# A vision layer's last image: the other image's tail on two banks, with a table of half-steps for each engine

## The reference

```
q, k, v = x Wq + bq, x Wk + bk, x Wv + bv
h = prelu((gamma * (q k^T)) v Wo + bo)            # no softmax
xm, gate = split(h W_in + b_in)                    # 128 each
xc = silu(xm W_conv + b_conv);  B, C = split(xc W_bc + b_bc)   # 16 each
dt = softplus(xc W_dt + b_dt)
scan over t, for 128 channels x 16 states:  s = exp(dt A) s + dt B xc ;  y = sum_states(C s)
h = layernorm(h + (y * silu(gate)) W_out + b_out)
# 16 groups of 64 tokens per image; each group has one of 16 experts and a shared one
f = relu(h Wi + bi);  twice: f = relu(f (W_expert + W_shared) + biases + f)
h = layernorm(h + f Wo + bo)
```

## Time and profile before

| | us |
|---|---|
| median of 3 runs | 341.44 (341.2, 341.44, 349.24) |
| profiled execution | 342.13 |
| its span | 339.7 |
| PE / PEld busy | 282.3 (83%) / 162.2 (48%) |
| DVE busy | 262.1 (77%) |
| ACT busy | 190.8 (56%) |
| POOL busy | 259.4 (76%) |
| DMA | 85.88 MB, mean 253 GB/s |
| TensorE's mean granted clock | 0.934 of full |

### The profile page before, as it was taken

One profiled execution on the slowest core, in us unless ns is written; L12 is line 12 of the kernel. 1 busy time (PEld: TensorE's weight loads), 2 busy tenths in 40 slices (PEclk: granted clock), 3 DMA queues, 4 the chain that ended last, 5 costly groups with the idle time before them and its releaser, 6 DMA issues. The chain is left out here.

```text
span 339.7 us, 4780 instructions
## 1 busy us (share of the span) xinstructions
PE 282.3 (83%) x1478; PEld 162.2 (48%) x1478; DVE 262.1 (77%) x287; ACT 190.8 (56%) x298; POOL 259.4 (76%) x136
## 2 busy tenths in 40 slices
PE   8898839875678689989797799997855999779996
PEld 5423412433336233356473243565644579458764
DVE  2565678998778988998898899987998799269420
ACT  3004831336895451679946525789377686657322
POOL 1028057999899989998998979989999999949300
PEclk9999957999698799999999799997898999979999
DMA  7970495686689997766799977668999999767000
GB/s 244 415 283 0 145 307 223 215 267 234 244 275 327 309 319 301 268 227 243 263 323 327 312 274 291 205 248 275 296 311 344 346 359 373 268 170 243 21 0 15
DMA packets 47128, 85.88 MB, mean 253 GB/s; under 512 B 7936, under 2 KB 24832, under 8 KB 46848
## 3 DMA queue, kind: packets, MB, share of 16 engines
q1 hardware_dynamic: 46704, 84.43, 73.9%
q10 hardware_dynamic: 400, 1.17, 1.1%
HBM read 75.62 MB, written 1.57 MB: 227 GB/s over the span
## 5 line engine op out<-in xcount | busy, mean ns | idle before, releaser
L1212 POOL TENSOR_TENSOR hc<-h,c_row 128x1024 f32<-128x1024 f32 (+1 forms) x79 | 154.6, 1967 | 22.4 <-DVE h L1341 19.4
L1201 POOL TENSOR_TENSOR ub<-u,b_row 128x1024 f32<-128x1024 f32 (+1 forms) x49 | 98.2, 2004 | 13.0 <-DVE u L1387 11.3
L925 ACT ACTIVATE decay<-delta,neg_a 128x512 f32<-128x512 f32 (+1 forms) x64 | 51.2, 811 | 62.6 <-DVE h L1341 62.2
L664 PEld LDWEIGHTS acc_y<-pack,hc 128*128 128x128 f32 x512 | 61.3, 147 | 39.3 <-issue 23.9
L664 PE MATMUL acc_y<-pack,hc 128*128 128x128 f32 x512 | 74.6, 286 | 3.1 <-POOL hc L1212 3.1
L1341 DVE TENSOR_TENSOR_SCAN h<-decay,ub 128x512 f32<-128x512 f32 (+1 forms) x41 | 66.0, 1610 | 14.4 <-ACT decay L925 7.3
L606 PE MATMUL work<-q,kT 64*128 64x512 f32 x112 | 36.0, 722 | 16.8 <-DVE mixed L1367 12.5
L1367 DVE TENSOR_TENSOR mixed<-gam,work 128x512 f32<-128x512 f32 x56 | 35.5, 676 | 7.2 <-PE work L606 6.6
L952 ACT ACTIVATE decay<-u 128x512 f32<-128x512 f32 (+1 forms) x42 | 26.4, 639 | 21.5 <-DVE h L1341 21.3
L617 PE MATMUL acc_r<-mixed,v_sb 128*64 128x512 f32 x128 | 37.0, 659 | 1.1 <-DVE mixed L1367 1.0
L1341 DVE TENSOR_TENSOR_SCAN h<-decay_own,decay 128x512 f32<-128x512 f32 (+1 forms) x23 | 34.5, 1498 | 1.1
(11 more groups left out here) (210 smaller groups left out, 357.9 us busy)
## 6 DMA issues: line engine op xcount, KB each, us to landing
b_row<-bc_dram SPq DMA_DIRECT2D x64, 512.0 KB, 5.1
c_row<-bc_dram SPq DMA_DIRECT2D x64, 512.0 KB, 5.8
group_w<-expert_w SPq DMA_DIRECT2D x48, 128.0 KB, 4.7
gam<-gammaT SPq DMA_DIRECT2D x8, 512.0 KB, 10.1
expert_w<-routed_w SPq DMA_DIRECT2D x1, 2048.0 KB, 17.9
gam<-expert_w SPq DMA_DIRECT2D x16, 128.0 KB, 5.3
x_in<-xT SPq DMA_DIRECT2D x4, 256.0 KB, 9.0
pack<-packed ACTq DMA_DIRECT2D x1, 788.0 KB, 6.5
```

Of the source, the lines that this page charges most:

```text
L664: mm = nc.tensor.matmul(acc_y[:, to:to + P], hc[:, at:at + P], ident, start=(job.state == 0 and c % 4 == 0), stop=(job.state == STATES - 1 ...
L925: op = nc.scalar.activation(target, delta[:, job.image % 2, columns], ACT.Exp, scale=neg_a[:, job.state:job.state + 1])
L1201: nc.gpsimd.tensor_tensor(ub[:, ring(made, job.halves)], u[:, job.image % 2, tokens(q)], b_row[:, ring(job.at, job.halves)], ALU.mult).the ...
L1212: nc.gpsimd.tensor_tensor(hc[:, here], h[:, here], c_row[:, here], ALU.mult).then_inc(hc_ready, job.halves)
```

## The change

Image 2 is now called `BESIDE`. Its tail leaves `last_steps` and gets a table for each engine: which uses are filled (TensorE), read by ScalarE, or read by VectorE in which half-step. Eight of its uses stay in the bank `tail`, five (`BESIDE_WORK`) move to the first bank of `work`, so that neighbouring uses alternate. Each fill of it first waits until the uses that its source comes from have been read.

In ScalarE's program the own decay of a half-step comes ahead of that half-step's tail work (it came behind it), and `y_out` and the reads of the tail follow. The first half's links are moved to later half-steps; its `out2`, `var2` and `rows` leave the loop and are woven between the links of the second half's tail, behind the last scan. The second half's third bank is the first bank of `slot`, free once scan 30 is done, and no longer the second of `work`. Warming matmuls after half-step 22 write to `acc_y`. The store of image 2's rows moves from n = 11 to n = 13 in SP's queue.

```diff
-TAIL_AT = (2, 3, 4, 5, 6, 7, 9, 10, 12, 13, 14, 15, 17, 18, 19, 20, 21, 22, 23)
-HALF_PE = {20: "y", 21: "out1", 22: "var1", 24: "f", 25: "layer1", 27: "layer2", 28: "out2", 29: "var2", 31: "rows"}
-HALF_ACT = {20: "y", 22: "square1", 23: "log1", 24: "f", 26: "layer1", 28: "layer2", 29: "square2", 30: "log2", 31: "rows"}
-HALF_DVE = {21: "y", 23: "var1", 30: "var2"}
+BESIDE = ALONE - 1
+BESIDE_TAIL = (USE_YT, USE_OUT1, USE_F0, USE_L1, USE_L2, USE_OUT2, USE_VAR2, USE_ROWS)
+BESIDE_WORK = (USE_YT + 1, USE_VAR1, USE_F0 + 1, USE_L1 + 1, USE_L2 + 1)
+BESIDE_PE = {
+    5: (USE_YT, USE_YT + 1), 7: (USE_OUT1,), 9: (USE_VAR1,), 12: (USE_F0, USE_F0 + 1), 14: (USE_L1,), 15: (USE_L1 + 1,),
+    16: (USE_L2,), 17: (USE_L2 + 1,), 19: (USE_OUT2,), 21: (USE_VAR2,), 24: (USE_ROWS,),
+}
+BESIDE_Y = 3
+BESIDE_ACT = {
+    7: (USE_OUT1,), 9: (USE_VAR1,), 12: (USE_F0, USE_F0 + 1), 14: (USE_L1,), 15: (USE_L1 + 1,), 16: (USE_L2,),
+    17: (USE_L2 + 1,), 19: (USE_OUT2,), 21: (USE_VAR2,), 24: (USE_ROWS,),
+}
+BESIDE_DVE = {5: (USE_YT,), 6: (USE_YT + 1,), 11: (USE_VAR1,), 23: (USE_VAR2,)}
+BESIDE_STORE = 13
+HALF_PE = {21: "y", 22: "out1", 24: "var1", 27: "f", 29: "layer1", 31: "layer2"}
+HALF_ACT = {19: "y", 22: "square1", 24: "log1", 27: "f", 29: "layer1", 31: "layer2"}
+HALF_DVE = {21: "y", 26: "var1"}
...
         def half_banks(g):
...
-            return slot[:, HALF:T], tail[:, :], work[:, HALF:T]
+            return slot[:, HALF:T], tail[:, :], slot[:, 0:HALF]
...
+            def fill_tail(b, use, part):
+                bank = tail_at(b, use)[0]
+                if part == WHOLE and use in (USE_OUT1, USE_OUT2):
+                    residual(b, use)
+                elif part == WHOLE:
+                    begin_tail(b, use)
+                if b == BESIDE:
+                    for source in TAIL_FROM.get(use, ()):
+                        pe.wait_ge(*tail_taken(b, source))
...
             def half_residual(g, bank):
...
-                    pe.wait_ge(half_out[0], 2)
+                    pe.wait_ge(scan_done, TOTAL - 1)
...
-                        if p == ALONE and 2 * n + i >= 24:
-                            if 2 * n + i == 24:
-                                pe.wait_ge(tail_read, TAIL_SETUP + TAIL_USES * ALONE)
-                            keep_warm(tail, 1)
+                        if p == ALONE and 2 * n + i >= 22:
+                            if 2 * n + i == 22:
+                                pe.wait_ge(half_y_read[0], 2)
+                            keep_warm(acc_y, 1)
                         for q in ended(start - 4, end - 4):
                             states_out(q)
                         if p == ALONE:
-                            for b, m in last_steps(p, n, i):
-                                last_part(b, m, LATE)
+                            for use in BESIDE_PE.get(2 * n + i, ()):
+                                fill_tail(BESIDE, use, WHOLE)
...
             def end_of_program():
-                half_residual(1, half_banks(1)[2])
                 for q in ended(TOTAL - 4, TOTAL - 2):
                     states_out(q)
-                pe.wait_ge(scan_done, TOTAL)
-                keep_warm(slot, 1)
+                half_residual(1, half_banks(1)[2])
+                keep_warm(acc_y, 1)
                 for q in ended(TOTAL - 2, TOTAL):
                     states_out(q)
-                keep_warm(slot, 1)
+                half_tail(0, "out2")
                 half_tail(1, "y")
-                keep_warm(slot, 1)
+                half_tail(0, "var2")
                 half_tail(1, "out1")
-                keep_warm(slot, 1)
+                keep_warm(acc_y, 1)
+                half_tail(0, "rows")
                 half_tail(1, "var1")
...
@@ ScalarE @@
                         for b, m in last_steps(p, n, i):
                             last_part(b, m)
-                        if p == ALONE and 2 * n + i in HALF_ACT:
-                            half_tail(0, HALF_ACT[2 * n + i])
                         for q in range(len(JOBS)):
                             if own_limit(start) <= JOBS[q].at < own_limit(end) and on_vector(q):
                                 own_decay(q)
+                        if p == ALONE:
+                            if 2 * n + i == BESIDE_Y:
+                                y_out(BESIDE)
+                            for use in BESIDE_ACT.get(2 * n + i, ()):
+                                take_tail(BESIDE, use)
+                            if 2 * n + i in HALF_ACT:
+                                half_tail(0, HALF_ACT[2 * n + i])
...
             def end_of_program():
                 half_tail(1, "y")
+                half_tail(0, "square2")
+                half_tail(0, "log2")
                 half_tail(1, "square1")
+                half_tail(0, "rows")
                 half_tail(1, "log1")
...
```

More of the change, by code:

```diff
@@ L294, in last_steps @@
                 steps.append((p - 2, n + STEPS))
-            if p == ALONE:
-                steps += [(p - 1, m) for m in range(LAST_STEPS) if TAIL_AT[m] == 2 * n + i]
-            elif i == 0 and 0 <= p - 1 < ALONE:
+            if i == 0 and 0 <= p - 1 < BESIDE:
                 steps.append((p - 1, n))
@@ L389, in tail_at @@
         def tail_at(b, use):
+            if b == BESIDE and use in BESIDE_WORK:
+                return (work[:, 0:HALF], work_full, work_read,
+                        FIRST_WORK_USES + WORK_USES * ALONE + BESIDE_WORK.index(use))
+            if b == BESIDE:
+                return tail[:, :], tail_full, tail_read, TAIL_SETUP + TAIL_USES * b + BESIDE_TAIL.index(use)
             return tail[:, :], tail_full, tail_read, TAIL_SETUP + TAIL_USES * b + use
@@ L470, in load_late_group, with store_rows @@
                     .then_inc(s_lw[g // 8], 16)
+            def store_rows(b):
+                sp.wait_ge(rows_ready, b + 1)
+                for g in range(2):
+                    sp.dma_start(out[b, g * HALF:(g + 1) * HALF, :].rearrange("(c t) d -> t c d", t=P),
+                                 res[:, :].rearrange("p (c i d) -> p i c d", d=D, i=2)[:, g, :, :]).then_inc(stored, 16)
             for p in PHASES:
@@ L503, in _ @@
                             load_group(p, g)
-                    for i in range(len(parts(p, n))):
-                        for b, m in last_steps(p, n, i):
[L506 to L511, removed]
+                    for b, m in last_steps(p, n, 0):
+                        if m == LAST_STEPS - 1:
+                            store_rows(b)
+                    if p == ALONE and n == BESIDE_STORE:
+                        store_rows(BESIDE)
             for g in range(2):
@@ L1030, in softplus_curve, with y_out, take_tail @@
                 nc.scalar.activation(delta[:, b % 2, :], delta[:, b % 2, :], ACT.Ln, bias=1.0).then_inc(sp_step, 1)
+            def y_out(b):
+                act.wait_ge(hc_used, 2 * STEPS * (b + 1))
+                nc.scalar.activation(y_t[:, :], acc_y[:, :], ACT.Copy).then_inc(y_read, 1)
             def last_part(b, n):
                 if n == 1:
-                    act.wait_ge(hc_used, 2 * STEPS * (b + 1))
-                    nc.scalar.activation(y_t[:, :], acc_y[:, :], ACT.Copy).then_inc(y_read, 1)
-                use = ACT_TAIL.get(n)
-                if b == ALONE - 1 and DVE_TAIL.get(n) in RELUS:
-                    use = DVE_TAIL[n]
-                bank = None if use is None else tail_at(b, use)[0]
+                    y_out(b)
+                if n in ACT_TAIL:
+                    take_tail(b, ACT_TAIL[n])
+            def take_tail(b, use):
+                bank = tail_at(b, use)[0]
                 if use in (USE_OUT1, USE_OUT2):
@@ L1458, in _ @@
                                 last_part(b, m)
+                            for use in BESIDE_DVE.get(2 * n + i, ()):
+                                take_tail(BESIDE, use)
                             if 2 * n + i in HALF_DVE:
```

115 lines of the change are left out of this document (56 added, 59 removed).

## The result

| | us |
|---|---|
| before, median of 20 runs | 343.38 (341.20 to 349.24) |
| changed kernel, median of 20 runs | 341.37 (337.58 to 346.44) |
| ratio | 0.9939, 95% interval 0.9917 to 0.9962 |
| a second measurement of the changed kernel | 339.67, ratio 0.9909, 0.9872 to 0.9946 |
| profiled execution of the changed kernel | 343.01, span 341.0, granted clock 0.925 |

The change is a gain of 2.0 us in the medians (2.1 by the ratio, 0.6%), where 3.8 were forecast, and the median lies 0.2 us above the range. The longer series of the kernel before also has a higher median than the three runs that the forecast stood on, by 1.9 us. The ratios in this document leave out runs more than 1.5% above the fastest of their kernel: three of the changed kernel's twenty, its profiled execution among them, four of e5's seven and four of e17's six.

The account below looks back on a forecast made before the run. PE's queue was taken to bound the last image, with ScalarE, DVE and POOL waiting behind it. The end's -4.1 us plus 0.3 behind y gave -3.8 us: 338.3 profiled, 337.6 median, range 334.3 to 341.2.

Parts of the forecast that it names:

- One hole before product 22: Sign of being right: POOL has one hole of 1.5 to 2.5 us before its product 22, none of 2 us before 24.
- Behind y: Step after the second half's y copy: the first half's out2, var2 and rows there cost 0.3 us, bounds -0.4 to +2.3.
- c_row: Row load in SP's queue: covered by 1.5 us; a POOL wait ended by it would show the forecast wrong.
- The end: Step from the first half's var1 to y on PE: y at 317.5 against 321.58, a gain of 4.1 us.
- PE idles some 2 us before f: In the step on the end: PE's wait before link f of the first half, some 2 us.
- I add 0.2 for an even chance of some of it: Clock term after the wait before f: 0.2 us for an even chance of some half-speed running.
- Two banks and the new half-steps: Step for image 2's tail on PE: OUT2 ends at 292.5 instead of 292.68, counted as no gain.
- the 33.07 us: PE's time from YT to the end of OUT2 in the kernel before, from which the forecast walked to 32.35.
- one wait of 0.45: PE's wait before F0, for image 2's first normalised values; taken in place of 0.74 us of idle.
- What two banks save is waiting ... and PE hardly waited: Claim that rotating banks gains nothing for image 2's tail, since PE was busy 21.56 of 22.00 us.
- The waits only move: Rival, chance 0.20: PE 1.7 us later at OUT2, scan 22 gains nothing, 1 to 2 us more behind y; 339.6 to 343.
- The slower rival: Rival, chance 0.04: PE drops to the lower clock in its full stretch, 270 to 292; 11 us slips, time 348.6.

Follow-up runs that it names:

- e5: Changed kernel without the five warming matmuls of half-steps 28 to 31 and between the residual and the last states; median 344.83 us, ratio 0.9897.
- e17: e13 with eight more warming matmuls in half-step 4's wait for image 2's y and three before link f; 342.08 us, ratio 0.9816.
- e16: Changed kernel with eight more warming matmuls on TensorE in half-step 4, in the wait for image 2's y; 339.28 us, ratio 0.9885.
- e3: Changed kernel with the first half's links at their old half-steps (var1 one later) and its out2, var2 and rows back in the loop; 343.47 us, ratio 0.9993.
- e6: Changed kernel with image 2's tail at the old half-steps on each engine, still on two banks; 341.44 us, ratio 0.9948.
- e19: Second run of e4 (changed kernel with four more warming matmuls before link f); 339.89 us, ratio 0.9894.
- e18: Changed kernel again without edits, as control beside e16, e17 and e19; 339.67 us, ratio 0.9909.
- e4: Changed kernel with four more warming matmuls on TensorE right before it waits for h1 at link f; 340.46 us, ratio 0.9915.
- e1: Changed kernel with all uses of image 2's tail back in the one bank `tail`; 347.0 us, ratio 1.0109.
- e10: Changed kernel with the edits of e4 and e5 together; 339.15 us, ratio 0.989.
- e2: Changed kernel with the last image's own decays back behind each half-step's tail work on ScalarE; 339.83 us, ratio 0.9899.
- e7: Changed kernel with image 2's y copied before the own decay and transposed before the rest of half-step 4 on TensorE; 340.1 us, ratio 0.9896.
- e13: Changed kernel with e7's edit plus the first half's y transposes ahead of image 2's second variance on TensorE; 336.65 us, ratio 0.9789.

## Why the prediction was wrong

**What held.** TensorE paces the stretch up to OUT2: with its clock kept up (e16) OUT2's square came 1.65 us earlier. OUT2 came at about the same time as before (41.68, forecast 41.2, before 41.44). One hole before product 22 of 1.5 to 2.5 us was forecast (2.61), none of size before 24 (0.26). PE has no gap from layer one to y, and y of the end is TensorE's: scan 31 ends at 62.52 and y comes at 68.54. Behind y 0.3 was forecast and 0.4 measured. c_row ended one short wait of POOL, 0.15 us at 264.87, and none from product 22 on. The gain comes from the links' later places, as e3 shows from the one side and e6 from the other.

**The step that failed is "The end", in its term for the clock.** "PE idles some 2 us before f" was right, 1.86; "I add 0.2 for an even chance of some of it" was not. The first half of layer one took 1.69 us for its eight passes instead of 1.00, a pair of warming matmuls and four transposes 1.06 each, and layer one with its centre product ended at 61.74 after the first scan instead of 59.6 forecast. With four warming matmuls in the gap, nothing else changed, y was 1.12 us earlier, and e19 repeats it (1.26 against e18). So where the clock falls the term is 1.1, not 0.2. The chance was near: in seven profiles with a wait of 1.85 or 1.86 us before f it fell in four. The price was not: 0.2 at even odds means 0.4 for a fall, and half of 1.1 would have been 0.55.

**A second term was the waits in "Two banks and the new half-steps".** TensorE's start was right to 0.1 us (8.95, forecast 8.9). Its first pieces ran at half speed, but so did as much of the same stretch in the kernel before, and the 33.07 us that the forecast took from there held it. What the walk had too small was its one wait of 0.45, for F0: the trace has 1.76 us of waits up to OUT2, 1.04 of them before F0, 0.28 before OUT1, 0.15 before VAR1 and 0.30 before the first expert fill. What it did not have at all is a gain: F0's two fills, now in one half-step and on two banks, ran side by side in 1.15 us, where before each took 1.02 to 1.05. So 1.31 us more waiting, 0.92 less for F0 and 0.07 of start make the 0.45 by which OUT2 came late. Scan 22 came 0.6, scan 24 0.9 and scan 31 1.1 later than walked; what adds up behind OUT2 I didn't take apart.

**The sum.** 2.3 us were missed at y: 0.9 up to f (it started at 55.22 after the first scan, forecast 305.6 less 251.27, or 54.3), 0.9 by the clock after it (1.1 less the 0.2 that I had), and 0.5 spread over ScalarE's relus and TensorE's queue from f to y, where e4, with the clock held, still needs 12.2 us and my walk had 11.7. By the profiles the change is then worth 70.31 - 68.54 - 0.4 = 1.4 us, by the ratios 2.1 and 3.1. They differ by less than the start of the first scan varies, and which is nearer can't be said from them. The time itself is 3.8 us above the forecast of 337.6, and 1.9 of that is no term of the change: the forecast stood on three runs of the kernel before, whose longer series has a median 1.9 us higher. On that base the same steps would have given 339.5, with 341.37 inside the range, and they would have been wrong all the same.

**"What two banks save is waiting ... and PE hardly waited" was right of the kernel before and wrong as a price.** The new tables need the second bank: without it the kernel is 1.1% slower than before, by e1's profile more through the clock behind the waits than through the waits. The page "Perfetto Trace Analysis" of the Trainium skill, section "Matmuls", whose rule on rotating banks I weighed against the row, holds here as a condition more than as a gain: e6 shows that with two banks the places in the tables are free; a two-bank kernel with the old links (e3) is where the kernel before was.

**The rival "The waits only move" has the measured time in its range, 339.6 to 343, and mostly by luck.** Its beginning came as it said, and further: DVE waited 3.40 us at half-step 5, scan 6 began at 13.92 after the first scan (12.23 before, 12.9 in that rival), and POOL had holes of 0.62 and 0.45 us there. But its condition did not come: OUT2 was 0.24 us later than before, not 1.7, scan 22 gained 1.0 and not nothing, and 0.4 us came behind y, not 1 to 2. The time came out there by the clock before layer one and the kernel before's higher median.

**The slower rival** did not come in the changed kernel: from 270 to 292, where TensorE works almost without gaps (20.51 of 22.00 us), the granted clock was 1.00. It came in the one-bank kernel, at that place and in a like way: a wait of 2.31 us until the bank was read, then 0.50 from 280 to 286. At the end e5 shows what it costs where it stays down, 4.5 us in one execution. The Trainium skill, page "TensorE: Matmul & The Clock Gate", section "A second HAM failure mode: psum-queue depth-cycling", lets the clock swing from cycling through banks; here it stayed up from 270 to 292 with the two-bank tail, and in the last image of all eighteen profiles every fall came in or behind a wait of TensorE, the shortest of 1.28 us (e10).

**What stays open.** The wait before f is 1.85 or 1.86 us in the changed kernel, e18, e2, e5, e16, e7 and e1. The clock fell after it in the first four and not in the last three. What decides it these runs don't show; nor how often it falls in runs without a profile. The store of image 2's rows at n = 13, the third bank in `slot` and the warming matmuls' new target were not run apart. The prices of the clock, 1.65 and 1.1 us, are those of profiles; no difference between runs confirms them beyond its interval.

## What to carry to other kernels

When several engines follow one table, ask which engine's queue is full and take out of it what others wait for: one swap in TensorE's order (y of the half before the variance that is wanted later) shortened the way from OUT2 to scan 22 by 1.3 us, where the whole change had brought scan 22 1.0 us forward. A wait on TensorE can cost twice, once for the time and once for the clock behind it; price a fall from the trace of before at each place where it waits, and only then weigh it with its chance. A comparison of two profiles holds only where their clocks agree: look at the mean granted clock of the stretch before giving its difference to the edit. And count from the last event that both kernels share: here it lay anywhere within 8 us, more than any of the effects.

## What was not expected

An own decay on ScalarE can stand on either side of the tail without harm that these runs show; and with TensorE never at half speed from the first scan on (e17) y came at 63.96, 6.4 us before the kernel before, while its ratio, 0.9816, is no better than e13's 0.9789.
